# Cross attention and a ternary feed-forward on one core: new lists of steps for the preparation, the first body and the steady body

## What is computed

```python
x = x + xattn(layernorm(x), ctx)      # one head of 512, keys and values from ctx
x = x + ffn(layernorm(x))

def xattn(m1, m2):
    x1, x2 = ln(m1, g1, b1), ln(m2, g2, b2)
    q, k, v = x1 @ Wq + bq, x2 @ Wk + bk, x2 @ Wv + bv
    return softmax(q @ k.T * 512 ** -0.5) @ v @ Wo + bo

def ffn(x):                           # hidden size 2048, rank 16
    h = bitlinear(x, w_fc) + gate * (x @ v.T @ fast_b.T @ u.T)
    return bitlinear(relu(h) ** 2, w_proj)

def bitlinear(x, w):
    scale = clip(mean(abs(w), axis=1), 1e-5)
    return x @ (clip(round(w / scale), -1, 1) * scale).T
```

## Time and profile before

| | us |
|---|---|
| median of 3 runs | 789.34 |
| lowest and highest | 788.86, 789.37 |
| the profiled execution, its own time | 789.24 |
| its span, first to last instruction | 787.4 |

### The profile page before, as it was taken

How to read it: one execution, slowest core, us unless ns; L and a number is a source line. 1 busy time by engine, 2 the same in 40 slices (tenths; PEclk the granted TensorE clock), 3 DMA queues, 4 the chain that set the end, 5 groups by cost and what they waited for, 6 DMA issues and landing times.

```text
span 787.4 us, 10870 instructions
## 1 busy us (share of the span) xinstructions
PE 773.5 (98%) x3877; PEld 645.0 (82%) x3877; DVE 563.1 (72%) x1128; ACT 376.2 (48%) x705; POOL 112.4 (14%) x143
## 2 busy tenths in 40 slices
PE   6999999999999999999999999999999999999997
PEld 4668788888888888888888888888888888888886
DVE  5998886778677687758777687768768687467434
ACT  5997455445443544345443545336443545324332
POOL 3242230110302002110302003110302003010001
PEclk9999999999999999999999999999999999999999
DMA  8743052154211531154210631154130730030101
GB/s 311 278 137 124 7 78 63 41 85 64 107 41 27 90 85 54 41 79 69 87 61 14 101 80 61 41 76 72 55 94 4 104 68 27 0 54 1 55 0 54
DMA packets 180554, 56.93 MB, mean 72 GB/s; under 512 B 167666, under 2 KB 168068, under 8 KB 180500
## 3 DMA queue, kind: packets, MB, share of 16 engines
q1 hardware_dynamic: 150368, 51.51, 26.7%
q10 hardware_dynamic: 30132, 4.73, 3.7%
...
## 4 chain that ended last, share of the span: by engine, by line
PE 94%; DVE 2%; DMA 2%; SPq 1%; issue 0%; ACT 0%; DVEq 0%
PE H L1352 30%; PE O L1333 29%; PE G L1217 25%; PE H L1358 4%; DMA Wv_s<-in_L_xattn_Wv_dram 2%; PE H L1201 1%; PE G L1299 1%; PE O L1406 1%; PE H L1217 1%; PE H L1194 1%; PE O L1373 1%; SPq L520 0%; PE G L1243 0%; PE O L1377 0%; DVE x2a L947 0%
## 5 line engine op out<-in xcount | busy, mean ns | idle before, releaser
L1333 PE MATMUL O<-projT,qbuf 128*128 128x512 f32 x992 | 241.8, 390 | 0.0
L1333 PEld LDWEIGHTS O<-projT,qbuf 128*128 128x128 f32 x992 | 184.8, 188 | 37.6
L780 ACT ACTIVATE rbuf<-H,scf 128x512 f32<-128x512 f32 x128 | 87.7, 686 | 112.3 <-PE H L1358 51.8
L788 ACT ACTIVATE qbuf<-rbuf 128x512 fp32r<-128x512 f32 x125 | 78.6, 629 | 125.0 <-PE O L1333 86.8
L1112 DVE TENSOR_TENSOR qbuf<-rbuf,qbuf 128x512 fp32r<-128x512 f32 x125 | 89.4, 715 | 67.6 <-ACT qbuf L788 66.6
L1352 PE MATMUL H<-even_group,fcT 128*128 128x512 f32 x512 | 126.8, 390 | 0.0
L1352 PE MATMUL H<-odd_group,fcT 128*128 128x512 f32 x512 | 126.7, 390 | 0.0
L1108 DVE TENSOR_TENSOR rbuf<-rbuf 128x512 f32<-128x512 f32 x128 | 95.7, 749 | 32.0 <-ACT rbuf L780 31.9
L1352 PEld LDWEIGHTS H<-odd_group,fcT 128*128 128x128 f32 x512 | 95.5, 188 | 19.5
L1352 PEld LDWEIGHTS H<-even_group,fcT 128*128 128x128 f32 x512 | 95.4, 188 | 19.3
L1217 PE MATMUL G<-Wvo,tT 128*128 128x512 f32 x270 | 63.0, 390 | 0.0
...
## 6 DMA issues: line engine op xcount, KB each, us to landing
xb<-in_x_dram SPq DMA_DIRECT2D x8, 1024.0 KB, 5.1
...
```

What stands on the lines that cost most here:

```text
L780: nc.scalar.activation(rbuf[:, j % 2, :], banks[f"H{j % 2}"][:, :], ACT.Relu, scale=scf[:, j:j + 1]).then_inc(relu_made, 1)
L788: nc.scalar.activation(squares(b, j)[:, HI, :], rbuf[:, j % 2, :], ACT.Copy).then_inc(sqhi_made, 1)
L1333: mm = pe.matmul(banks[f"O{t}"][:, :], qbuf[:, j % 2, h, t * P:(t + 1) * P], projT[:, j, :], start=(j == 0 and h == HI), stop=(j == NFF - ...
```

## The change

The lists of PROLOGUE, BODY_ORDER and FIRST_ORDER are written in another order, on all engines; LAST_ORDER is untouched. Each list holds the same steps as before, each engine does the same work, and the same code runs for each step. On SP the order of the loads changes: Wq:2, ring:0, Wq:1, Wq:0, Wq:3 come first, ring:8 to ring:11 go ahead of Wv or of ctx, and ctx goes behind Wv. In the preparation turn:28 to turn:31 and nx0+ to nx3+ are spread over the end; in FIRST_ORDER down:0 and down:1 go ahead of up:3; in BODY_ORDER t:0 goes ahead of down:0. Since the order of the jobs on PE (JOBS) stays, so do their banks.

```diff
--- before.py
+++ after.py
@@ -115,49 +115,49 @@
 
 BODY_ORDER = {
     "pe": (
-        "down-:14 L:0 up:0 down-:15 up:1 up:2 up:3 down:0 down:1 t:0 t:1 up:4 t:2 up:5 down:2 s:0 up:6 s:1 s:2 down:3 "
-        "pT:0 s:3 up:7 down:4 up:8 pT:1 down:5 w:0 w:1 up:9 w:2 down:6 up:10 a:0 a:1 a:2 a:3 down:7 up:11 down:8 "
-        "up:12 up:13 down:9 down:10 up:14 down:11 down:12 up:15 down:13 "
+        "down-:14 L:0 up:0 down-:15 up:1 up:2 up:3 up:4 t:0 down:0 down:1 t:1 t:2 up:5 s:0 s:1 down:2 up:6 s:2 up:7 "
+        "pT:0 down:3 s:3 down:4 pT:1 up:8 w:0 down:5 up:9 w:1 w:2 down:6 a:0 a:1 a:2 a:3 down:7 up:10 up:11 down:8 "
+        "up:12 down:9 down:10 up:13 up:14 down:11 up:15 down:12 down:13 "
     ).split(),
     "act": (
-        "L:0 up:0 n1hi0 n1hi1 hi:0 up:1 n1hi2 n1hi3 up:2 hi:1 up:3 n2hi0 t:0 t:1 hi:2 n2hi1 n2hi2 t:2 up:4 hi:3 up:5 "
-        "n2:0 n2:1 hi:4 s:0 n2:2 s:1 s:2 n2:3 hi:5 pT:0 up:6 s:3 up:7 pT:1 hi:6 hi:7 w:0 up:8 w:1 w:2 up:9 nx0+ nx1+ "
-        "hi:8 nx2+ hi:9 nx3+ up:10 up:11 xmove:12 xmove:13 xmove:9 hi:10 xmove:10 xmove:14 xmove:11 up:12 hi:11 "
-        "xmove:8 xmove:15 up:13 hi:12 nc0+ up:14 hi:13 xhi0 xhi1 nc1+ hi:14 up:15 xhi2 xhi3 hi:15 nc2+ nc3+ "
+        "L:0 up:0 n1hi0 up:1 hi:0 n1hi1 n1hi2 up:2 hi:1 n1hi3 up:3 t:0 n2hi0 n2hi1 t:1 hi:2 n2hi2 t:2 hi:3 n2:0 n2:1 "
+        "up:4 s:0 hi:4 n2:2 up:5 s:1 n2:3 s:2 up:6 pT:0 s:3 hi:5 pT:1 hi:6 up:7 hi:7 w:0 up:8 w:1 w:2 up:9 nx0+ nx1+ "
+        "nx2+ hi:8 nx3+ xmove:14 xmove:13 hi:9 up:10 xmove:11 xmove:8 hi:10 up:11 xmove:15 xmove:9 xmove:12 xmove:10 "
+        "hi:11 up:12 hi:12 up:13 xhi0 up:14 hi:13 nc0+ nc1+ xhi1 xhi2 nc2+ hi:14 up:15 xhi3 nc3+ hi:15 "
     ).split(),
     "dve": (
-        "L:0 n1raw0 n1raw1 n1raw2 n1raw3 sq:0 out01 out23 sq:1 n1lo0 lo:0 n1lo1 n1lo2 lo:1 sq:2 n1lo3 n2raw0 n2raw1 "
-        "outsum01 sq:3 t:0 outsum23 lo:2 n2lo0 n2raw2 t:1 n2lo1 n2lo2 t:2 lo:3 sq:4 s:0 s:1 s:2 lo:4 sq:5 n2:0 pT:0 "
-        "n2:1 sq:6 s:3 lo:5 sq:7 n2:2 n2:3 xs01+ pT:1 cs01+ w:0 lo:6 xs23+ w:1 w:2 lo:7 sq:8 sq:9 cs23+ a:0 lo:8 a:1 "
-        "a:2 nX0 a:3 lo:9 nX1 nX2 nX3 sq:10 lo:10 sq:11 sq:12 lo:11 lo:12 sq:13 xraw0 xraw1 sq:14 xraw2 lo:13 lo:14 "
-        "xlo0 xraw3 sq:15 xlo1 xlo2 xlo3 lo:15 "
+        "L:0 n1raw0 n1raw1 n1lo0 out01 sq:0 n1raw2 lo:0 n1lo1 sq:1 n1raw3 n1lo2 n1lo3 out23 sq:2 lo:1 n2raw0 t:0 "
+        "n2raw1 sq:3 n2raw2 outsum01 n2lo0 t:1 n2lo1 n2lo2 t:2 lo:2 outsum23 n2:0 sq:4 lo:3 s:0 n2:1 s:1 s:2 lo:4 "
+        "n2:2 pT:0 sq:5 n2:3 s:3 lo:5 pT:1 sq:6 lo:6 sq:7 xs01+ lo:7 w:0 sq:8 xs23+ w:1 w:2 cs01+ sq:9 a:0 a:1 a:2 "
+        "a:3 nX0 nX1 nX2 nX3 lo:8 sq:10 lo:9 lo:10 sq:11 cs23+ lo:11 sq:12 lo:12 xraw0 xraw1 xraw2 sq:13 xlo0 lo:13 "
+        "sq:14 xraw3 lo:14 xlo1 xlo2 sq:15 xlo3 lo:15 "
     ).split(),
     "pool": (
-        "residual xs23+ a:0 a:1 cs23+ a:2 a:3 "
+        "residual xs23+ a:0 a:1 a:2 a:3 cs23+ "
     ).split(),
 }
 
 
 FIRST_ORDER = {
     "pe": (
-        "up:3 down:0 down:1 up:4 up:5 down:2 up:6 down:3 up:7 t:0 t:1 down:4 t:2 up:8 s:0 down:5 s:1 s:2 down:6 pT:0 "
-        "s:3 up:9 pT:1 down:7 w:0 w:1 w:2 up:10 a:0 a:1 a:2 a:3 up:11 down:8 up:12 down:9 down:10 up:13 up:14 down:11 "
-        "up:15 down:12 down:13 "
+        "down:0 down:1 up:3 up:4 up:5 down:2 up:6 t:0 t:1 t:2 down:3 down:4 s:0 s:1 up:7 s:2 pT:0 down:5 s:3 down:6 "
+        "pT:1 up:8 up:9 w:0 down:7 w:1 w:2 up:10 a:0 a:1 a:2 a:3 down:8 up:11 up:12 down:9 up:13 down:10 up:14 "
+        "down:11 down:12 up:15 down:13 "
     ...
     ).split(),
     "dve": (
-        "sq:2 sq:3 lo:2 n1raw0 sq:4 n1raw1 n1raw2 n1lo0 lo:3 n1raw3 n1lo1 n1lo2 n1lo3 sq:5 lo:4 sq:6 t:0 lo:5 n2raw0 "
-        "n2raw1 t:1 n2raw2 n2lo0 n2lo1 n2lo2 t:2 xs01+ s:0 n2:0 lo:6 sq:7 n2:1 s:1 s:2 lo:7 n2:2 pT:0 s:3 n2:3 pT:1 "
-        "xs23+ w:0 sq:8 w:1 w:2 sq:9 lo:8 lo:9 sq:10 a:0 a:1 a:2 nX0 a:3 nX1 nX2 nX3 cs01+ sq:11 lo:10 cs23+ sq:12 "
-        "lo:11 lo:12 sq:13 xraw0 xraw1 sq:14 lo:13 xlo0 xraw2 lo:14 xraw3 xlo1 xlo2 xlo3 sq:15 lo:15 "
+        "sq:2 n1raw0 n1raw1 lo:2 sq:3 n1lo0 n1raw2 lo:3 n1raw3 n1lo1 n1lo2 n1lo3 sq:4 n2raw0 t:0 n2raw1 lo:4 n2lo0 "
+        "n2raw2 sq:5 n2lo1 n2lo2 t:1 t:2 lo:5 xs01+ s:0 n2:0 s:1 sq:6 xs23+ s:2 n2:1 lo:6 sq:7 pT:0 s:3 lo:7 n2:2 "
+        "n2:3 pT:1 w:0 sq:8 lo:8 sq:9 w:1 w:2 lo:9 a:0 a:1 nX0 a:2 nX1 sq:10 a:3 nX2 nX3 lo:10 sq:11 lo:11 cs01+ "
+        "sq:12 cs23+ lo:12 sq:13 sq:14 xraw0 lo:13 xlo0 xraw1 xraw2 xraw3 lo:14 xlo1 xlo2 xlo3 sq:15 lo:15 "
     ...
@@ -202,39 +202,40 @@
 
 PROLOGUE = {
     "sp": (
-        "Wq:1 Wq:0 ring:0 ring:1 ring:2 ring:3 Wq:2 Wq:3 ring:4 Wk:1 Wk:0 g2row bqrow Wk:2 x:0 ring:5 ctx:0 ring:6 ring:7 "
-        "Wv:0 ring:8 ring:9 ring:10 ring:11 ring:12 ring:13 ring:14 ring:15 ring:16 bo ring:17 ring:18 ring:19 "
-        "ring:20 lowrank ring:21 ring:22 ring:23 ring:24 ring:25 ring:26 ring:27 ring:28 ring:29 ring:30 ring:31 next "
+        "Wq:2 ring:0 Wq:1 Wq:0 Wq:3 ring:1 ring:2 ring:3 g2row Wk:0 ring:4 Wk:2 bqrow ring:5 Wk:1 x:0 ring:6 ring:7 "
+        "ring:8 ring:9 Wv:0 ring:10 ring:11 ctx:0 bo ring:12 ring:13 lowrank ring:14 ring:15 ring:16 ring:17 ring:18 "
+        "ring:19 ring:20 ring:21 ring:22 ring:23 ring:24 ring:25 ring:26 ring:27 ring:28 ring:29 ring:30 ring:31 next "
     ).split(),
     "pe": (
-        "wqT:0 wqT:1 vecs wqT:2 wqT:3 bq:0 turn:0 wkT:0 turn:1 wkT:1 wkT:2 turn:2 M:0 M:1 turn:3 wvT:0 wvT:1 n1T:0 "
-        "n1T:1 M:2 turn:4 turn:5 bv:0 turn:6 turn:7 wvT:2 n1T:2 wvo:0 turn:8 turn:9 n1T:3 turn:10 turn:11 wvo:1 wvo:2 "
-        "turn:12 turn:13 turn:14 n2T:0 turn:15 co:0 M:3 n2T:1 turn:16 fb:0 n2T:2 n2T:3 turn:17 turn:18 turn:19 t:0 "
-        "t:1 t:2 turn:20 turn:21 ut:0 turn:22 s:0 s:1 s:2 pT:0 s:3 ut:1 turn:23 ut:2 turn:24 pT:1 ut:3 w:0 w:1 w:2 "
-        "turn:25 turn:26 turn:27 a:0 a:1 a:2 a:3 turn:28 turn:29 turn:30 turn:31 x:0 x:1 x:2 x:3 sprow B.L:0 "
-        "B.up:0 B.up:1 B.up:2 "
+        "vecs wqT:0 wqT:1 wqT:2 wqT:3 bq:0 wkT:0 turn:0 wkT:1 wkT:2 turn:1 turn:2 M:0 M:1 turn:3 wvT:0 turn:4 turn:5 "
+        "n1T:0 wvT:1 n1T:1 M:2 bv:0 turn:6 turn:7 n1T:2 wvT:2 wvo:0 n1T:3 turn:8 wvo:1 turn:9 n2T:0 turn:10 turn:11 "
+        "wvo:2 n2T:1 turn:12 turn:13 turn:14 n2T:2 turn:15 co:0 M:3 turn:16 turn:17 n2T:3 fb:0 turn:18 turn:19 t:0 "
+        "t:1 t:2 turn:20 turn:21 ut:0 s:0 s:1 s:2 turn:22 pT:0 s:3 ut:1 turn:23 ut:2 turn:24 turn:25 pT:1 ut:3 w:0 "
+        "w:1 w:2 turn:26 turn:27 a:0 a:1 a:2 turn:28 a:3 x:0 x:1 turn:29 sprow x:2 turn:30 x:3 B.L:0 B.up:0 B.up:1 "
+        "turn:31 B.up:2 "
     ).split(),
     "act": (
-        "abs:0 abs:1 vecs abs:2 abs:3 wqT:0 wqT:2 wqT:3 store:0 abs:4 store:1 store:2 tb abs:5 Wo M:0 abs:6 abs:7 M:1 "
-        "nx0 nx1 wvT:0 wvT:1 abs:8 nx2 abs:9 abs:10 n1T:0 n1T:1 store:3 M:2 abs:11 abs:12 store:4 abs:13 abs:14 "
-        "abs:15 store:5 nc0 wvT:2 nx3 store:6 store:7 n1T:2 n1T:3 wvo:0 nc1 abs:16 abs:17 store:8 store:9 abs:18 "
-        "abs:19 abs:20 store:10 store:11 wvo:1 wvo:2 store:12 nc2 abs:21 abs:22 n2T:0 abs:23 store:13 store:14 "
-        "store:15 n2T:1 nc3 M:3 fb:0 n2T:2 n2T:3 abs:24 abs:25 store:16 store:17 abs:26 abs:27 store:18 store:19 uhi "
-        "t:0 t:1 t:2 store:20 abs:28 n2:0 ut:0 store:21 n2:1 s:0 s:1 n2:2 s:2 pT:0 abs:29 n2:3 ut:1 s:3 store:22 pT:1 "
-        "ut:2 store:23 abs:30 abs:31 ut:3 w:0 w:1 w:2 store:24 store:25 store:26 store:27 store:28 store:29 diag "
-        "x:0 x:1 x:2 x:3 nx0+ nx1+ nx2+ nx3+ B.L:0 sprow_out B.up:0 B.hi:0 B.up:1 store:30 store:31 B.hi:1 nc0+ nc1+ nc2+ nc3+ "
+        "vecs abs:0 wqT:0 abs:1 abs:2 abs:3 wqT:2 wqT:3 store:0 abs:4 abs:5 tb abs:6 abs:7 M:0 abs:8 store:1 Wo M:1 "
+        "nx0 nx1 wvT:0 n1T:0 store:2 wvT:1 abs:9 store:3 nx2 n1T:1 M:2 abs:10 abs:11 store:4 nx3 store:5 abs:12 "
+        "store:6 abs:13 store:7 wvT:2 n1T:2 abs:14 wvo:0 n1T:3 nc0 nc1 abs:15 abs:16 store:8 nc2 store:9 abs:17 "
+        "abs:18 store:10 n2T:0 wvo:1 abs:19 wvo:2 store:11 store:12 n2T:1 nc3 store:13 store:14 abs:20 abs:21 n2T:2 "
+        "store:15 M:3 abs:22 n2T:3 abs:23 fb:0 store:16 abs:24 store:17 abs:25 uhi store:18 abs:26 t:0 t:1 abs:27 "
+        "store:19 abs:28 t:2 store:20 n2:0 ut:0 n2:1 n2:2 s:0 s:1 store:21 s:2 pT:0 n2:3 store:22 ut:1 ut:2 s:3 "
+        "abs:29 pT:1 abs:30 abs:31 w:0 store:23 ut:3 w:1 store:24 w:2 store:25 nx0+ diag nx1+ store:26 store:27 nx2+ "
+        "nx3+ store:28 x:0 store:29 x:1 sprow_out x:2 x:3 B.L:0 store:30 B.up:0 B.hi:0 B.up:1 store:31 nc0+ B.hi:1 "
+        "nc1+ nc2+ nc3+ "
     ).split(),
     "dve": (
-        "wqT:1 bqacc sides:0 sides:1 sides:2 bq:0 wkT:0 wkT:1 wkT:2 xs01 xs23 cs01 sides:3 M:0 M:1 sides:4 tern:5 "
-        "sides:6 tern:7 cs23 n1T:0 n1T:1 M:2 bv:0 tern:8 tern:9 tern:10 sides:11 sides:12 tern:13 wvo:0 sides:14 "
-        "tern:15 coacc n1T:2 n1T:3 wvo:1 wvo:2 tern:16 sides:17 sides:18 co:0 sides:19 n2T:0 n2T:1 M:3 n2T:2 n2T:3 "
-        "uprep fb:0 tern:20 sides:21 sides:22 sides:23 ulo t:0 t:1 t:2 sides:24 sides:25 n2:0 s:0 s:1 s:2 sides:26 "
```

(20 more changed lines are left out.)

## The result

| | before | changed |
|---|---|---|
| median of the runs | 789.37 us (788.86 to 789.88, 5 runs) | 792.63 us (792.43 to 793.14, 5 runs) |
| span of the profiled execution | 787.4 us | 790.6 us |
| start of the first body's own work on PE | 101.38 | 104.28 |
| period of a steady body, mean of five | 89.45 | 89.53 |

The ratio is 1.0041, with a 95% interval of 1.0030 to 1.0052: the change costs 3.3 us where I forecast a gain of 1.5. That is outside my range, 786.4 to 789.9.

What follows compares the result with a forecast made beforehand. PE, busy 773.5 of 787.4 us, bounds the kernel, so gains lie only ahead of 101.4 us. Terms -0.2 and -1.2 give -1.4 from 789.24, forecast 787.9 us as median; range 786.4 to 789.9.

Steps and rivals of the forecast that it cites:

- Part 1: Loads and first jobs, 0 to 17 us: M:0 0.5 us late, then a balance of -0.2 at wvT:0.
- part 3: End of the preparation, 78 to 101 us: a:0 starts 1.2 us earlier, waits at x:1 and x:3 shrink; -1.2 us.
- Part 2: Preparation, 23 to 78 us, PE, DVE and ACT nearly full: reordering takes 0 for the whole, t:0 level again.
- opening and full stretch lose: Rival, first part of the preparation: ctx, Wo or the ACT list late, +1.0 to +2.0, 789.0 to 789.9 us; chance 0.12.
- The two small terms for nx ahead of L:0: End of the preparation: ACT does nx before x:0, gaining about 0.3 us at L:0 and 0.1 at up:0.
- turn:31 with what stands around it: End of the preparation: turn:31 still to be paid behind up:1 on PE, costing 0.44 us.
- Part 4: First body: down:0 and down:1 ahead of up:3 find their inputs ready, t:0 its lists; 0 us.
- Part 5: Six steady bodies: copy and subtraction fit behind up:5 and down:6, period of 89.45 us kept; 0 us.
- My margin of 0.2 at a:0: Steady body: DVE finishes w:2 0.2 us before PE asks, with down:6 (1.81 us) between a:0 and w:2.
- Stall rival: Steady body at a:0: late DVE chain makes PE stand 0.5 us in each of six, 790.9 us; chance 0.11.
- The clock rival: Opening: PE's clock rises only after M:0 has begun, costing about 1.3 us, result 789.2; chance 0.06.

Runs made afterwards that it cites:

- both meetings repaired: Changed kernel with sides:2 back ahead of bq:0 and sides:17 to sides:19 ahead of co:0 on DVE; 789.55 us, ratio 1.0003.
- the run with the old body: Changed kernel with sides:2 ahead of bq:0, sides:17 to sides:19 ahead of co:0 on DVE, and BODY_ORDER of before; 789.05 us, ratio 0.9994.
- the two kernels with the end alone: Kernel before with new PE, ACT and DVE lists from sides:29 and a:0 on: 794.5 us; also with POOL's B.xs23 ahead of a:0: 788.63 us.

## Why the prediction was wrong, point by point

- **Part 1, the loads: right, and not what mattered.** bqrow landed as worked out, PE began at 5.33 where I had 6.3, and M:0 was forecast 0.5 late. The failed term is "behind bqrow ... M:0 starts at about 17.6". That sum has room for sides:2 at its usual length and no more (0.8 for two instructions, as part 3 prices sides:31); at its new place it cost 1.12 + 1.48. M:0 came at 19.15. Moving it back brings 17.01, moving it alone costs the kernel before 1.9 us.
- **Part 2, the full stretch: the step that failed most.** I went "down the new lists with the durations of the old timeline", and took PE, DVE and ACT, but not POOL, which at 14% busy seemed free to be shuffled. I wrote of the bodies that "the pool lists only trade places", and of the preparation's POOL list nothing at all. t:0 was to be within 0.5 of 53.8, and came at 57.41. With both meetings repaired it comes at 54.43, and at 53.93 in the run with the old body: the rest of my sum for this part, zero, holds. The price of the meetings at t:0 is 57.41 - 54.43 = 3.0 us. The "opening and full stretch lose" rival (0.12) had the direction, at most +2.0, and named ctx, Wo and ACT; none of these was late, for PE shows no wait between M:0 and the second meeting.
- **Part 3, the end: right in mechanism, about half in size.** The waits at x:1 and x:3 are gone. I had 1.4 with the 0.2 of part 1, so 1.2 here; it was 0.72. Counted from t:0, DVE's a:0 came 1.3 us earlier (81.80 - 53.79 = 28.01 before, 84.12 - 57.41 = 26.71), where I had 1.2. The mis-sized term is what stands behind it, "The DVE chain of four a and the nX is otherwise the same": from a:0 to the end of nX3 it took 10.02 us and not 9.66, so x:3 came 0.94 earlier and not 1.25. DVE now reaches a:0 and a:1 before PE has made them, and the two are 2.04 us apart, before 1.81. nX3 in the kernel before, then a:0, a:1 and nX3 in the changed one:

```profile
90.91 0.55 DVE L1096 TENSOR_SCALAR nrm<-x2a,nmv,nrs 128x512 f32<-128x512 f32 x1 [0.43 <-PE H L1243]
```

```profile
84.12 0.75 DVE L948 SCALAR_TENSOR_TENSOR x2a<-G,rinv,x2a 128x512 f32<-128x512 f32 x1 [0.18 <-PE G L1218]
...
86.16 0.75 DVE L948 SCALAR_TENSOR_TENSOR x2a<-H,rinv,x2a 128x512 f32<-128x512 f32 x1 [0.15 <-PE H L1218]
...
93.59 0.55 DVE L1097 TENSOR_SCALAR nrm<-x2a,nmv,nrs 128x512 f32<-128x512 f32 x1 [0.43 <-POOL nrs L655]
```

The two small terms for nx ahead of L:0 gave 0.3 of their 0.4 (from x:3 to up:1 5.36 us, before 5.68), and turn:31 with what stands around it cost 0.54 and not 0.44 (from up:1 to the first body's work 4.64 us, before 4.10). In the two kernels with the end alone a:0 came only 0.8 earlier from t:0 (at 81.60 and 81.30, t:0 at 54.37 and 54.10).
- **Part 4, the first body: right.** From its first work to the end of the program the repaired kernel with the old steady body takes 786.7 - 100.77 = 685.9 us, and the kernel before 686.0. The new first body costs nothing.
- **Part 5, steady bodies: near.** My margin of 0.2 at a:0 held; no body stalls. But the body isn't free: 0.08 us each, 0.5 for six. The rows show only a part of where it lies. The four groups of a take 8.18 or 8.19 us (8.21 in one body), with the old body 8.16; and both transposes of p are now followed by products of 512 columns, 1.93 and 1.94 us for a group that otherwise takes 1.84, where one of them was followed by products of 256 columns, 1.15 for a usual 1.07. The rest stays open. Stall rival: didn't happen.
- **The clock rival fell for the changed kernel.** The turns at 13.79 us start 0.055 apart, a little before the place where the earlier trace rows has it.
- **The sum.** By stretch I had -0.2 up to t:0, -1.2 from there to the first body, and 0 behind it. The spans show +3.6, -0.7 and +0.3. Of the +3.6, 3.0 are the two meetings. The rest, 0.6, is no more than t:0 varies by between traces with the old lists up to there: 53.79 in the kernel before, 54.10, 54.37 and 54.46 in three others. One trace of the changed kernel can't be told from that. The +0.3 behind the preparation is the price of six bodies, 0.5, less 0.2 that I can't place.
